# Softmax loop of a graph kernel: sixteen slots for gathered rows, given free by VectorE's update

## The reference

```
h = features @ W.T + b
s1 = h @ a1_w + a1_b[0]
s2 = h @ a2_w + a2_b[0]
src = edge_index[0]
dst = edge_index[1]
e = s1[src] + s2[dst]
e = jnp.where(e >= 0, e, NEG_SLOPE * e)
m = jax.ops.segment_max(e, src, num_segments=n)
ex = jnp.exp(e - m[src])
denom = jax.ops.segment_sum(ex, src, num_segments=n)
att = ex / denom[src]
out = jax.ops.segment_sum(att[:, None] * h[dst], src, num_segments=n)
```

## Time and profile before

| what | value |
|---|---|
| median of three runs | 3019.51 us (3010.88 to 3020.82) |
| the profiled execution's own time | 2996.43 us |
| its span in the trace | 2994.6 us |
| DVE busy over the span | 2350.5 us (78%) |
| PE busy over the span | 2386.8 us (80%) |
| POOL busy over the span | 2000.6 us (67%) |
| gathers of the softmax loop (L546) | 832, 943 ns each on average |

### The profile page before, as it was taken

One profiled execution on the slowest core, in us unless ns is written; L12 is line 12 of the kernel. 1 busy time (PEld: TensorE's weight loads), 2 busy tenths in 40 slices (PEclk: granted clock), 3 DMA queues, 4 the chain that ended last, 5 costly groups with the idle time before them and its releaser, 6 DMA issues. The chain is left out here.

```text
span 2994.6 us, 44539 instructions
## 1 busy us (share of the span) xinstructions
PE 2386.8 (80%) x11705; PEld 1541.4 (51%) x11705; DVE 2350.5 (78%) x5910; ACT 1525.4 (51%) x4524; POOL 2000.6 (67%) x1839
## 2 busy tenths in 40 slices
PE   5899999999999999999997366666666666666662
PEld 2355555555555555555555355555555555555551
DVE  8899999999999999999999455555554555555557
ACT  0366666666666666666665334343343433443433
POOL 0388788778887888888785566666666666666660
PEclk9999999999999999999999665566655666666665
DMA  2233333333333333333332323332232222333322
GB/s 87 67 98 99 95 97 98 99 99 96 97 97 99 98 97 96 96 99 99 99 95 63 79 67 69 65 69 66 65 68 66 68 66 66 69 67 67 66 61 47
DMA packets 156606, 244.12 MB, mean 82 GB/s; under 512 B 40837, under 2 KB 84399, under 8 KB 156227
## 3 DMA queue, kind: packets, MB, share of 16 engines
q0 software_dynamic: 58624, 108.72, 16.7%
q1 hardware_dynamic: 97730, 132.55, 15.3%
HBM read 231.99 MB, written 9.12 MB: 81 GB/s over the span
## 5 line engine op out<-in xcount | busy, mean ns | idle before, releaser
L503 POOL DMA_INDIRECT room<-in_x,pks x784 | 1013.5, 1293 | 351.8 <-issue 238.3
L546 POOL DMA_INDIRECT room<-h_rows,idx x832 | 785.0, 943 | 476.6 <-issue 457.6
L798 PE MATMUL FP<-fc_sb,room 128*128 128x512 f32 x1568 | 834.5, 613 | 4.5 <-DMA room<-in_e 4.5
L597 ACT ACTIVATE w_sb<-WP 128x512 f32<-128x512 f32 x784 | 468.1, 597 | 502.6 <-PE WP L807 306.0
L885 PE MATMUL FP<-ident,room 128*128 128x128 f32 x1664 | 385.8, 405 | 359.2 <-DMA room<-h_rows,idx 224.8
L807 PE MATMUL WP<-at_p,rel_oh 100*128 100x512 bf16 x2352 | 637.7, 379 | 1.7 <-issue 1.7
L885 PEld LDWEIGHTS FP<-ident,room 128*128 128x128 f32 x1664 | 332.4, 297 | 410.6 <-DMA room<-h_rows,idx 255.2
L682 ACT ACTIVATE accT<-accT,neg_big 128x512 f32<-128x512 bf16 x208 | 150.0, 721 | 762.6 <-DVE accT L1263 417.1
L807 PEld LDWEIGHTS WP<-at_p,rel_oh 100*128 100x128 bf16 x2352 | 228.3, 97 | 546.9 <-issue 452.4
L1111 DVE TENSOR_TENSOR z<-FP,w_sb 128x1024 f32<-128x1024 f32 x392 | 479.9, 1224 | 20.8 <-issue 12.3
L1118 DVE SCALAR_TENSOR_TENSOR y<-z 128x2048 f32<-128x2048 f32 x196 | 447.9, 2285 | 0.0
(11 more groups left out here) (222 smaller groups left out, 3071.2 us busy)
## 6 DMA issues: line engine op xcount, KB each, us to landing
room<-in_e SPq DMA_DIRECT2D x196, 256.0 KB
rel_sb<-in_rel_g SPq DMA_DIRECT2D x196, 200.0 KB
z<-sorted_sources SPq DMA_DIRECT2D x208, 128.0 KB
room<-h_rows,idx POOLq DMA_INDIRECT x832
room<-in_x,pks POOLq DMA_INDIRECT x784
sorted_edges<-runs,ridx POOLq DMA_INDIRECT x196
accT<-in_x_t SPq DMA_DIRECT2D x1, 3125.0 KB, 9.8
h_rows<-arena SPq DMA_DIRECT2D x13, 227.5 KB, 2.8
```

The costliest lines, as they stand in the source:

```text
L503: pool.indirect_dma_start(xg[:, k, u, 0:P], None, x[:, :], bass.IndirectOffsetOnAxis(ap=pks[:, k, u:u + 1], axis=0)).then_inc(xg_in[k], 16)
L546: pool.indirect_dma_start(hg[k][:, u, :], None, h_dram[:, :], bass.IndirectOffsetOnAxis(ap=idx1[:, k, u:u + 1], axis=0)).then_inc(g_in[k], 16)
L597: nc.scalar.activation(w_sb[:, u // 2, u % 2, :], WP[u % 2][:, :], ACT.Copy).then_inc(w_copied, 1)
L798: mm = pe.matmul(FP[u // 2][:, u % 2, :], e_sb[:, k, u, :], fc_sb[:, :], start=True, stop=True)
```

## The change

S1 goes from 8 to 16. The eight new slots lie in `arena`, in the columns that held `h_sb` until it was written to DRAM; because PE still reads the last column of `h_sb` once (`n_s1t`), POOL's first gather also waits for that. A slot is now given free by `st_ready` (DVE's `update`), not by `o_done` (PE's `attend`). ACT writes row numbers AHEAD = 11 groups ahead. The count of groups is rounded up to a multiple of 16 instead of 8, which gives 208 with these inputs as before. The parts that are unrolled with a register are 16 groups long, and on DVE the loop body has 16 groups instead of 4.

```diff
-G1 = 8 * -(-(G0 + NS) // 8)
-G1_LEAST = 8 * -(-G0 // 8)
+S1 = 16
+G1 = S1 * -(-(G0 + NS) // S1)
+G1_LEAST = S1 * -(-G0 // S1)
...
-S1 = 8
 LAG = 5
-AHEAD = 5
-D1 = 4
+AHEAD = 11
+IN_ROOM = 8
+G_IN = 16 * TG // S1
...
-        hg_all = room[:, 0:S1 * TG * HROW].rearrange("p (s u k) -> p s u k", s=S1, u=TG)
-        hg = [hg_all[:, k, :, :] for k in range(S1)]
+        hg = [f[:, j * TG * HROW:(j + 1) * TG * HROW].rearrange("p (u k) -> p u k", u=TG)
+              for f, n in ((room, IN_ROOM), (arena, S1 - IN_ROOM)) for j in range(n)]
...
             def group1(g, k, lead):
                 pool.wait_ge(i1_ready, g + 1)
                 if not lead:
-                    pool.wait_ge(o_done, g - S1 + 1)
+                    pool.wait_ge(st_ready, g - S1 + 1)
...
             more = group_count(pool)
+            pool.wait_ge(n_s1t, 1)
             for k in range(S1):
                 group1(k, k, True)
...
             def idx(g, k, lead):
                 if not lead:
-                    act.wait_ge(g_in[k], 16 * TG + (g - k - S1) * 8)
+                    act.wait_ge(g_in[k], 16 * TG + (g - k - S1) * G_IN)
...
-            with dve.Fori(G1_LEAST - S1, dve.snap(more + (G1_LEAST - 2 * S1 + D1 + 1)), D1) as i:
-                half = dve.snap(i & (S1 - D1))
-                other = dve.snap(S1 - 2 - half)
-                for k in range(D1):
-                    step1(i + k, k, False, half + k, half + (k - 2) if k >= 2 else other + k)
+            with dve.Fori(G1_LEAST - 2 * S1, dve.snap(more + (G1_LEAST - 2 * S1 + 1)), S1) as i:
+                for k in range(S1):
+                    step1(i + k, k, False, k, (k - 2) % S1)
```

More of the change, by code:

```diff
@@ L194, in build @@
         mT = accT[:, 0:SLOTS * GE // 2].bitcast(BF16).rearrange("p (s k) -> p s k", s=SLOTS)
-        pen = accT[:, S1 * GE // 2:S1 * GE // 2 + SLOTS * GE].rearrange("p (s k) -> p s k", s=SLOTS)
-        hg_all = room[:, 0:S1 * TG * HROW].rearrange("p (s u k) -> p s u k", s=S1, u=TG)
-        hg = [hg_all[:, k, :, :] for k in range(S1)]
+        pen = accT[:, SLOTS * GE:2 * SLOTS * GE].rearrange("p (s k) -> p s k", s=SLOTS)
+        hg = [f[:, j * TG * HROW:(j + 1) * TG * HROW].rearrange("p (u k) -> p u k", u=TG)
+              for f, n in ((room, IN_ROOM), (arena, S1 - IN_ROOM)) for j in range(n)]
         z_flat = z[:, 0, :, :].rearrange("p a k -> p (a k)")
@@ L218, in build @@
         ge = msg_flat[0:NS, 2 * G1:3 * G1]
-        s1_parts = msg_flat[:, TG * HROW:TG * HROW + 2 * G1].bitcast(BF16)[:, 0:G1 * PARTS3].rearrange(
+        s1_parts = msg_flat[:, TG * HROW:TG * HROW + 3 * G1 // 2].bitcast(BF16)[:, 0:G1 * PARTS3].rearrange(
             "p (g c) -> p g c", c=PARTS3)
@@ L472, in _ @@
             more = group_count(sp)
-            for g in range(RSLOTS, G1_LEAST):
+            for g in range(RSLOTS, G1_LEAST - S1):
                 sources(g, g % S1, False)
-            with sp.Fori(G1_LEAST, sp.snap(more + (G1_LEAST - S1 + 1)), S1) as i:
+            with sp.Fori(G1_LEAST - S1, sp.snap(more + (G1_LEAST - S1 + 1)), S1) as i:
                 for k in range(S1):
@@ L549, in _ @@
             more = group_count(pool)
+            pool.wait_ge(n_s1t, 1)
             for k in range(S1):
                 group1(k, k, True)
-            for g in range(S1, G1_LEAST):
+            for g in range(S1, G1_LEAST - S1):
                 group1(g, g % S1, False)
-            with pool.Fori(G1_LEAST, pool.snap(more + (G1_LEAST - S1 + 1)), S1) as i:
+            with pool.Fori(G1_LEAST - S1, pool.snap(more + (G1_LEAST - S1 + 1)), S1) as i:
                 for k in range(S1):
@@ L725, in _ @@
                 step1(k, k, True)
-            for g in range(S1, G1_LEAST - S1):
+            for g in range(S1, G1_LEAST - 2 * S1):
                 idx(g + AHEAD, (g + AHEAD) % S1, False)
@@ L729, in _ @@
                 step1(g, g % S1, False)
-            with act.Fori(G1_LEAST - S1, act.snap(more + (G1_LEAST - 2 * S1 + 1)), S1) as i:
+            with act.Fori(G1_LEAST - 2 * S1, act.snap(more + (G1_LEAST - 2 * S1 + 1)), S1) as i:
                 for k in range(S1):
@@ L879, in rows @@
             def rows(g, k, lead):
-                pe.wait_ge(g_in[k], 16 * TG + (g - k) * 8)
+                pe.wait_ge(g_in[k], 16 * TG + (g - k) * G_IN)
                 if k >= 2 or not lead:
@@ L922, in _ @@
                 step1(k, k, True)
-            for g in range(S1, G1_LEAST - S1):
+            for g in range(S1, G1_LEAST - 2 * S1):
                 step1(g, g % S1, False)
-            with pe.Fori(G1_LEAST - S1, pe.snap(more + (G1_LEAST - 2 * S1 + 1)), S1) as i:
+            with pe.Fori(G1_LEAST - 2 * S1, pe.snap(more + (G1_LEAST - 2 * S1 + 1)), S1) as i:
                 for k in range(S1):
@@ L1285, in edge_sum @@
                 v.tensor_tensor(el[:, 0, :], sm[:, :, 0],
-                                hg_all[:, bass.ds(at, 1), :, P + 1].rearrange("p o u -> p (o u)"),
+                                hg[at][:, :, P + 1],
                                 ALU.add).then_inc(edge_summed, 1)
```

## The result

The changed kernel takes 3102.47 us (median of 4 runs, 3099.96 to 3114.56) against 3017.56 us for the kernel before, measured beside it (4 runs, 3010.88 to 3020.82): ratio 1.0295, 95% interval 1.0275 to 1.0315, so 85 us slower. The profiled execution took 3103.44 us, its span is 3101.6.

What follows compares the result with a forecast made beforehand. It took the softmax loop to be bound by POOL's gathers plus stops for PE's late signals. First burst -12, restart and row numbers +48, end +30 gave +66 on the 3019.5 us median: 3085 us, range 2975 to 3130.

Steps and rivals of the forecast that it cites:

- later restarts and a longer end: Main forecast for the softmax loop: POOL restarts later after stops, longer tail after the last gather; 3085 us, chance 0.56.
- Depth: Softmax loop: rows ready up to nine steps early end PE's 188 us of waiting; gain 0 to 188 us, 0 taken.
- First burst: Start of the softmax loop: 64 gathers in one burst instead of 32, then one stop; gain 12 us, bounds 0 and 18.
- Restart and row numbers: POOL's stops: waiting for DVE's update and ACT's row numbers lengthens them; 0.25 us per group, +48 us, bounds 0 and 69.
- The end: From last gather to last update: DVE further behind, 50 us instead of 21.0; loss taken as +30 us, 20 to 42.
- `n_s1t`: Before POOL's first gather: this wait lies beside the one for `h_rows`; nothing taken, up to 2 us.
- The reading under it: Softmax loop: PE's signals arrive late during unbroken gathers and come through after the last has landed; unpriced, called no proof.
- The rule that spoke against it: SBUF: DMA and engine traffic use disjoint ports and cannot slow each other, so late signals would not come from gathers.
- POOL alone sets the pace: Rival for the softmax loop: all stops go, 5.0 us a group, 192 us less; about 2825 us, chance 0.12.

Runs made afterwards that it cites:

- Experiments 1 and 2: Changed kernel with slots freed by PE's `o_done` again: 3079.84 us, ratio 1.0224; changed kernel with AHEAD 13 instead of 11: 3066.64 us, ratio 1.0176.
- Experiment 3: Kernel before, eight slots, with a slot freed by DVE's update instead of PE's `o_done`: 3045.20 us in one run on a holding chip.
- experiment 4: Kernel before with only two of a group's four tiles gathered from the ninth group on: 2467.95 us in one run, 544 less.
- 9: Changed kernel itself, unaltered, measured beside the kernel before on a free chip: 2784.61 us, ratio 1.0020.
- both repairs: Changed kernel with slots freed by PE's sums and row numbers 13 groups ahead: 2786.77 us, ratio 1.0018; repeated, 2785.02 us, ratio 1.0021; free chips.
- the broadcasts: Kernel before without SyncE's broadcasts of a group's local numbers behind the fourth group: 2781.35 us on a free chip, kernel before 2781.55.

## Why the prediction was right, and where its sizes were off

The forecast, 3085 us by later restarts and a longer end, is what happened: 3102, in the range. It happened on a holding chip, the kind that the rows of before came from; on a free chip the change costs 5.5 us where I forecast 66. That the result came from the same kind of chip as the rows of before was luck, in so far as I knew of no other kind. Term by term, in profiled executions. The one of before lies 21 us below its median and the one of after 1 above, so what follows adds up to 107 us, not 85; I put the excess down to the loop, since the rest repeats within a microsecond or three; no second profile of the kernel before on a holding chip shows it.

- **Depth, 0.** Right. PE's wait for rows vanished and bought nothing. The releases still come behind POOL's bursts.
- **First burst, -12.** Too large: -2.5. The 64 gathers stood in one burst (but for one pause of 1.8 us before the sixteenth group, where a row number is all that POOL can wait for), yet the stop behind it was 14.4 us instead of some 6, and it was a row number that ended it: DVE and ACT had made so few steps in 80 us that ACT was not at the number needed. So my argument that row numbers come before 80 us are over failed twice here. The 64 gathers and their stop took 95.7 us; before, the same groups took 98.2. I had priced this stop at one release and one update.
- **Restart and row numbers, +48.** The mechanism was right, the size short. Over the next 176 groups the rate went from 6.02 to 6.44 us a group, +74 us; less the 20 us by which that profile of before ran fast, it is some 54, 0.3 a group, and I had taken 0.25 within a bound of 0.36. POOL's gather comes 1.1 us behind the start of DVE's update, where it was 0.61: the 0.5 us that I had priced. But stops of 3.7 us (37, ended by an update) and 5.5 (25, ended by a row number, without the first) stand for my 2.9 to 4.5, and bursts are of twelve nearly throughout, where I had eight to twelve. Experiments 1 and 2 divide it: PE's signal gives some 21 us back, earlier row numbers some 36, each with some 4 us of it at the end of the loop.
- **The end, +30.** 47.8 us against 21.0, +26.8. Right; the ten last steps ran at 3.3 us. Experiment 3 keeps 21.1 us with eight slots, so it comes with the depth. On a free chip it is nothing (20 us with sixteen slots, 21 with eight), as DVE isn't behind there.
- **`n_s1t`, 0.** The loop began 3.1 us later; but over all traces the first gather starts at 1667.6 to 1669.8 us in kernels that have that wait and at 1666.7 to 1669.7 in kernels that don't, so nothing can be told.
- **A term that I had not.** The span ends 12.9 us after the last output transfer is issued, where it was 7.8:

```profile
2986.80 0.53 SPq L487 DMA_DIRECT2D out_x<-arena  x1
```

```profile
3088.70 0.52 SPq L488 DMA_DIRECT2D out_x<-arena  x1
```

  (before, span 2994.6; after, span 3101.6). Every kernel with sixteen slots has 12.7 to 13.2 us there and every one with eight, on either kind of chip, 6.9 to 7.9, those with the wait for `n_s1t` included. On free chips these 5 us are nearly all of the 5.5 us that the change costs. The profile shows no instruction in them. What they are I didn't try.

**The reading under it**, that PE's signals are late while gathers follow without a break, I had called a reading. What is shown now: on a holding chip the loop needs 3.35 us a step when POOL gathers half as much and rests 2 us behind every four gathers (experiment 4), and on a free chip all gathers, with no rest, hold nothing up (9). So the holding goes with two things, gathers in long unbroken bursts and a certain kind of chip. And it is wider than I had it: not PE's signals alone come late, but also those that DVE gives to itself, so "PE's sum is heard late" is one case of it. These traces cannot tell a signal that travels late from an engine that takes note of it late, or from an instruction that itself reaches its engine late.

The rule that spoke against it was the Trainium skill's, SBUF — State Buffer, section on SBUF's two separate sides. Nothing here speaks against it as far as the work itself goes: a gather takes 0.94 us and DVE's maximum 0.68 us on both kinds of chip. What I drew from it, that late signals would then not come from the gathers, does not hold on the holding chip: there, in one run, DVE's steps went from slow to fast when the gathers became fewer and spaced. And the rival "POOL alone sets the pace", priced at 2825 us, is what free chips do, the changed kernel in 2784.61 us and the kernel before in 2779.14.

**What stays open.** What in a holding chip keeps the signals back, and whether the same chip can be holding at one time and free at another. Whether a short pause of POOL lets the signals through, whether both repairs together bring sixteen slots level with eight, and whether the broadcasts play a part: each has been measured on a free chip only. No version here that computes the right output beats the kernel before.

## What to carry to other kernels

A queue of prepared work helps only the engine that waits for work. Where the late thing is a signal, a longer queue adds a backlog at its end (27 us here) and can lengthen the way back from consumer to producer, and nothing covers either. When the producer is released by another engine's step, look at what else that same step must bring (here the row numbers), and let it come a step or two sooner.

And compare a kernel on more than one chip before explaining its stops: a run on a second chip would have shown that 8% of this kernel's time, and all but 5 us of this change's cost, depend on where (or when) it runs and not on the program alone.

## What the hardware showed that I had not expected

- The kernel before took 3017.6 and 3011.7 us in two comparisons and 2781.6, 2779.1, 2779.3 and 2778.2 in four others, these on four different chips. Within a comparison it repeats within 0.4%; only the profiled execution of before, 2996.43 us, lies further off. The whole difference lies in this loop: with eight slots the first gather starts at 1666.7 to 1669.7 us on both kinds, and the last one 71 to 73 us before the end of the span.
- On a holding chip and under a burst of gathers DVE waited up to 3.8 us for a signal that it had given itself.
- On a free chip 832 gathers follow each other every 1.25 us, with never more than 0.3 us between two.
- A memset of 64 columns on POOL takes 0.17 us and costs 0.75 us a time where POOL sets the pace; the next gather, which waits for it, starts 0.81 us after its end.
